# Attention a: statistics of two norms side by side, one GpSimd power for both, the second norm applied behind the maximum, the router later

## Chip, core and metric

One core of a Trainium2 chip runs the whole kernel. The metric is the device time of one execution in microseconds (us). Engines: PE is TensorE, PEld its weight loads, DVE is VectorE, ACT is ScalarE, POOL is GpSimd, SP is SyncE (here it only issues DMAs).

## What is computed

The input is 16 blocks of 256 tokens with 128 features. Four layers follow each other, each with a residual:

```
x = x + attn_a(layernorm(x))     # one head of width 128, rotary table, softmax over the 256 keys
x = x + ffn(layernorm(x))        # router: 8 experts, the best one per token, gate = its softmax value
x = x + attn_b(layernorm(x))     # 16 heads of width 64, causal
x = x + ffn(layernorm(x))        # the same experts again

def _layernorm(x, eps=1e-05):
    m, v = mean(x), var(x)
    return (x - m) / sqrt(v + eps)
```

## The kernel before

The kernel is written for each engine as one queue of instructions in program order, with semaphores between them. X holds all tokens on chip (128 tokens by 128 features a tile, two tiles a block). There are four stages: attention a with the router of the first expert layer (up to about 147 us), the experts, attention b with the second router, and the experts again.

Attention a is a software pipeline over the blocks. In turn s every engine runs its `attn_a(s, u)`, which does a different step for each of several blocks: the first norm (A) of block s, projections and rotary product of block s-1, scores, maximum and exponentials of s-2, transposed probabilities and output of s-3, residual and second norm (F) of s-4, the router of s-5. `has(b)` asks whether the block exists. Turns 0 to 7 are written out, 8 to 13 are a loop of two turns a round, then follow the routing of the first eight blocks (`route(0)`), turns 14 to 20, and the routing of the other eight (`route(1)`) with the experts.

The order in each queue in a turn of before:

- VectorE: residual of s-4 (L603); statistics (L558), aggregate (L565) and variance (L570) of norm A; the same of norm F; reciprocal of the row sums (L618); apply of A, called lnA, and of F, called lnF (both L581); rotation product (L630); maximum over the keys (L635); its scaling (L638); rotary sum (L644); router logits (L588).
- GpSimd: power -0.5 of A's variance, then of F's (L313), then the sine product of the rotary table (L351). In turns 14 to 19 each is followed by three scatters (L318) of routed tokens.
- ScalarE: copy of the transposed norm, xnT (L421); the router's copies TOK (L410) and fT (L413); copy of the transposed probabilities (L429); copy for the sine product (L434); two exponentials with row sums (L441); copy of the values, va (L449).
- TensorE: transposes of lnA (L902); router transposes of lnF (L885); transposes of the probabilities (L916); projections (L928); scores (L936); values (L943); output (L953); router products (L891).

In turns 17 to 20 a weight part is added: ScalarE casts (L488) and VectorE subtracts (L770).

`then_inc` raises a semaphore at an instruction's end, and `wait_ge` holds the whole queue of its engine. For instance, the second norm is applied under this wait:

```
b = s - 4
if has(b):
    norm_apply(LN["F"], b, TPB * b, u)     # dve.wait_ge(ln["s_rstd"], n + 1), two tensor_scalar
```

Of the kernel before, what the change touches and what calls it, by code (L numbers as in the profile page):

```python
# [111 lines left out]
def build(nc, ids, x, wqk_a, wv_a, rope, w_q, w_k, wv_b, w_o, W1, b1t, W2, b2, Wr, br, cst, out):  # L112
    ctx = ExitStack()
    with ctx:
# [17 lines left out]
        onesb = sb("onesb", [P, P], BF16)  # L132
        half = sb("half", [P, TPB])
        WQK = sb("WQK", [P, 4, D])
# [9 lines left out]

        LN = {}
        for n in "AFB":
            LN[n] = {
                "stats": sb(f"stats{n}", [P, 2, TPB, 6]), "mv": sb(f"mv{n}", [P, 2, TPB, 2]),
                "var": sb(f"var{n}", [P, 2, TPB]), "rstd": sb(f"rstd{n}", [P, 2, TPB]),
                "out": LN["A"]["out"] if n == "B" else sb(f"ln{n}", [P, 2, TPB, D]),  # L150
                "s_stats": sem(f"ln{n}_stats"), "s_mv": sem(f"ln{n}_mv"), "s_var": sem(f"ln{n}_var"),
                "s_rstd": sem(f"ln{n}_rstd"), "s_out": sem(f"ln{n}_out"),
            }
# [150 lines left out]
        def _(pool):  # L304
# [6 lines left out]
            def rstd(ln, n, slot):  # L311
                pool.wait_ge(ln["s_var"], n + 1)
                nc.gpsimd.tensor_tensor(ln["rstd"][:, slot, :], ln["var"][:, slot, :], half[:, :],  # L313
                                        ALU.pow).then_inc(ln["s_rstd"], 1)
# [25 lines left out]
            def attn_a(s, u):  # L340
                if has(s):
                    rstd(LN["A"], s, u)
                if has(s - 4):
                    rstd(LN["F"], s - 4, u)
                b = s - 1
                if has(b):
                    pool.wait_ge(a_qks, b + 1)
                    wait(pool, a_rope, b)
                    if fixed(b) and b == 0:
                        pool.wait_ge(s_wa, 48)  # L350
                    nc.gpsimd.tensor_tensor(rot[:, 1, :], qks[:, :], ROPE[:, 1, :], ALU.mult).then_inc(a_sin, 1)  # L351

            peeled(attn_a, 0, 8)
            turns(pool, attn_a, 8, 14)
            for s in range(14, NB + 5):
# [50 lines left out]
        def _(act):  # L406
# [8 lines left out]
            def attn_a(s, u):  # L415
                v = (u + 1) % 2
                b = s - 1
                if has(b):
                    act.wait_ge(a_xT_ps, b + 1)
                    wait(act, a_v_ps, b - 1)  # L420
                    nc.scalar.copy(xnT[:, v, :], PS[:, 4, 0:M]).then_inc(a_xT, 1)  # L421
                b = s - 5
                if has(b):
                    router_copies(b, TPB * b, v, 7)
                b = s - 3
# [20 lines left out]
                if has(b):  # L446
                    act.wait_ge(a_v_ps, b + 1)
                    wait(act, a_out_ps, b - 1)
                    nc.scalar.copy(va[:, v, :, :], PS[:, 5, 0:TPB * D].rearrange("p (t d) -> p t d", t=TPB)).then_inc(a_v, 1)  # L449

            def route(k):
# [80 lines left out]
            turns(act, attn_a, 14, 16)  # L532
            for s in range(16, NB + 5):
                attn_a(s, s % 2)
                if s >= NB + 1:
                    weight_parts(s - (NB + 1))
# [11 lines left out]
        def _(dve):  # L548
# [23 lines left out]

            def norm_stats(ln, n, tile, slot):
                bn_stats(ln, n, tile, slot)
                bn_aggr(ln, n, slot)
                norm_var(ln, n, slot)

            def norm_apply(ln, n, tile, slot):
                dve.wait_ge(ln["s_rstd"], n + 1)
# [12 lines left out]
            def attn_a(s, u):  # L592
# [14 lines left out]
                if has(s):  # L607
                    if not fixed(s) or s >= 2:
                        dve.wait_ge(a_xT_ps, s - 1)
                    norm_stats(LN["A"], s, TPB * s, u)  # L610
                if has(b):
                    dve.wait_ge(a_x, b + 1)
                    wait(dve, r_tok, b - 1)
                    norm_stats(LN["F"], b, TPB * b, u)
                b = s - 3
# [3 lines left out]
                if has(s):  # L619
                    norm_apply(LN["A"], s, TPB * s, u)  # L620
                b = s - 4
                if has(b):
                    norm_apply(LN["F"], b, TPB * b, u)
                b = s - 1
                if has(b):
# [3 lines left out]
                    wait(dve, a_rope, b)  # L629
                    nc.vector.tensor_tensor(rot[:, 0, :], PS[:, 0, :], ROPE[:, 0, :], ALU.mult).then_inc(a_rot, 1)  # L630
                b = s - 2
                if has(b):
# [4 lines left out]
                    dve.wait_ge(a_max, b + 1)  # L637
                    nc.vector.tensor_scalar(nba[:, u, :], mxa[:, u, :], -SCALE_A, None, ALU.mult).then_inc(a_nb, 1)  # L638
                b = s - 1
                if has(b):  # L640
# [4 lines left out]
                                            ALU.add).then_inc(a_rope, 1)  # L645
                b = s - 5
                if has(b):
                    if fixed(b) and b == 0:
                        dve.wait_ge(s_wr, 32)
                    logits(b, TPB * b, 7)  # L650

# [130 lines left out]
            def attn_b(s, u, p0=0, p1=NPAIR):  # L782
# [8 lines left out]
                for p in range(p0, p1):  # L791
# [26 lines left out]
                    if p == 4 and has(s):  # L818
                        norm_apply(LN["B"], s, TPB * s, u)
                    if p == 4 and has(fb):  # L820
# [9 lines left out]
                    if p == 5 and has(fb):  # L830
                        norm_apply(LN["F"], fb + NB, TPB * fb, u)
                    if has(b):
# [16 lines left out]
            turns(dve, attn_a, 14, 16)  # L849
            for s in range(16, NB + 5):  # L850
                attn_a(s, s % 2)
                if s >= NB + 1:
                    weight_parts(s - (NB + 1))
# [19 lines left out]
        def _(pe):  # L873
# [21 lines left out]
            def attn_a(s, u):  # L895
                v = (u + 1) % 2
                b = s - 1
                if has(b):
# [4 lines left out]
                    last.then_inc(a_xT_ps, 1)  # L903
                b = s - 5
                if has(b):
                    if fixed(b) and b == 0:
                        pe.wait_ge(s_wr, 32)
                    wait(pe, r_lg, b)
                    router_T(b, v, 7)
                b = s - 3  # L910
# [21 lines left out]
                if has(b):  # L932
                    pe.wait_ge(a_rope, b + 1)
                    wait(pe, a_exp, b)
                    for i in range(TPB):
                        last = mm(PS[:, 2, i * M:(i + 1) * M], qk[:, u, 0, i * P:(i + 1) * P], qk[:, u, 1, :],  # L936
                                  start=True, stop=True)
                    last.then_inc(a_scores, 1)
                b = s - 1
                if has(b):  # L940
# [6 lines left out]
                if has(b):  # L947
# [161 lines left out]
            turns(pe, attn_a, 14, 16)  # L1109
            for s in range(16, NB + 5):  # L1110
                attn_a(s, s % 2)
# [77 lines left out]
```

## Time and profile before

| | |
|---|---|
| median of 3 runs | 983.93 us (983.05 to 984.64) |
| profiled execution | 987.06 us |
| its span | 984.9 us |
| granted TensorE clock, mean | 0.934 |
| busy: PE, DVE, ACT, POOL | 86%, 66%, 57%, 45% |

The span runs from the first to the last instruction; the 2.2 us around it are start and end of the execution. In a row in order of time, the first number is the start in us from the span's start, the second the duration, and what stands in square brackets is the idle time of the engine before it with what ended it. "x2" means two instructions taken together. The name before the arrow is the tile written. XY and w1b are tiles that attention a borrows: XY holds probabilities and copies there, w1b the rotated products.

### The profile page before, as it was taken

The page shows a single profiled execution, that of the slowest core. Times are in us where ns is not written, and L with a number is a line of the kernel's source. Part 1 is how long each engine was busy: PE and PEld are TensorE (multiplying, and loading weights), DVE is VectorE, ACT ScalarE, POOL GpSimd, SP SyncE. Part 2 cuts the span into 40 slices and gives each one's busy share as a digit, 9 for nine tenths or more (in the row PEclk, how much of TensorE's full clock was granted, in tenths as well). Part 3 has the DMA queues.
Part 4 walks back from the last instruction along what each step waited for, and adds up shares of the span by engine and source line. Part 5 has one row for each costly group of instructions (what it writes and reads, how often), then busy time and mean ns, then how long its engine had stood idle before and what let it go on. Part 6 is the DMA issues. An engine that isn't in the chain of part 4 may idle for free. (4 is left out here: it accounts for less than half of the span.)

```text
span 984.9 us, 24722 instructions
## 1 busy us (share of the span) xinstructions
PE 843.6 (86%) x6756; PEld 706.2 (72%) x6756; DVE 645.8 (66%) x2713; ACT 557.7 (57%) x2089; POOL 441.0 (45%) x755
## 2 busy tenths in 40 slices
PE   5888665399979999999999979989999999538993
PEld 4676555399967778777877857867877787538993
DVE  4888866166647776776767687667667666615665
ACT  2444343166657766776676656666667666315661
POOL 3333362555534444443434424674444444074552
PEclk9999777599979999999999999999999999768996
DMA  9900012302010000000000000001000000021214
GB/s 335 320 14 0 9 36 78 105 32 78 32 52 2 1 2 2 2 2 2 1 2 1 0 1 2 18 29 62 0 1 0 0 2 1 4 99 41 78 35 144
DMA packets 25936, 40.05 MB, mean 41 GB/s; under 512 B 4656, under 2 KB 17584, under 8 KB 24816
## 3 DMA queue, kind: packets, MB, share of 16 engines
q1 hardware_dynamic: 20848, 28.76, 9.0%
q0 software_dynamic: 4992, 10.27, 3.2%
q8 instruction: 29, 0.48, 0.2%
q14 instruction: 67, 0.55, 0.2%
HBM read 20.58 MB, written 18.43 MB: 40 GB/s over the span
## 5 line engine op out<-in xcount | busy, mean ns | idle before, releaser
L378 POOL TENSOR_SCALAR pb<-pb,rib 128x128 f32<-128x128 f32 x256 | 96.0, 375 | 307.1 <-DVE rib L789 306.0
L804 DVE CUSTOM_DVE_ANT_0 PS<-PS,CST 128x128 f32<-128x128 f32 (+1 forms) x512 | 167.8, 389 | 62.0 <-PE PS L1022 49.6
L473 ACT ACTIVATE yT<-PS,w1b 128x128 f32<-128x128 f32 x368 | 105.3, 369 | 115.7 <-remote 48.1
L503 ACT COPY qk<-PS 128x512 f32<-128x512 f32 x128 | 75.1, 587 | 155.6 <-PE PS L880 155.6
L334 POOL DMA_INDIRECT yt_dram<-XY x92 | 97.8, 1063 | 82.0 <-DVE XY L737 78.4
L840 DVE COPY pT<-PS 128x384 f32<-128x384 f32 x256 | 130.6, 551 | 1.8 <-PE PS L1033 1.1
L1022 PE MATMUL PS<-qk 64*128 64x128 f32 (+1 forms) x1024 | 120.0, 353 | 8.2 <-ACT pb L520 6.6
L520 ACT ACTIVATE pb<-PS,nbb 128x256 f32<-128x256 f32 x256 | 125.3, 490 | 0.0
L380 POOL TENSOR_SCALAR pb<-pb,rib 128x256 f32<-128x256 f32 x256 | 123.2, 481 | 0.0
L1001 PE MATMUL PS<-yT 128*128 128x128 f32 x736 | 102.9, 285 | 20.8 <-ACT yT L473 12.8
L1033 PE MATMUL PS<-CST,pb 128*128 128x128 f32 x768 | 110.8, 277 | 10.8 <-POOL pb L380 9.9
L1043 PE MATMUL PS<-pT,vb 128*64 128x256 f32 (+1 forms) x1024 | 111.5, 339 | 0.0
L1001 PEld LDWEIGHTS PS<-yT 128*128 128x128 f32 x736 | 94.4, 201 | 22.3 <-ACT yT L473 13.8
L992 PE MATMUL PS<-pb,w1b 128*128 128x128 f32 x736 | 105.7, 290 | 0.2 <-issue 0.2
L518 ACT ACTIVATE pb<-PS,nbb 128x128 f32<-128x128 f32 x256 | 97.9, 382 | 9.3 <-DVE nbb L804 9.0
L1033 PEld LDWEIGHTS PS<-CST,pb 128*128 128x128 f32 x768 | 87.8, 143 | 17.7 <-POOL pb L380 17.4
L992 PEld LDWEIGHTS PS<-pb,w1b 128*128 128x128 f32 x736 | 96.6, 205 | 0.9 <-issue 0.3
L789 DVE RECIPROCAL rib<-rsb 128x2 f32<-128x2 f32 x256 | 40.9, 160 | 81.4 <-ACT pb L520 80.8
L737 DVE TENSOR_TENSOR XY<-PS,yT 128x128 f32 (+1 forms) x92 | 26.8, 292 | 98.6 <-PE PS L1001 48.6
L1043 PEld LDWEIGHTS PS<-pT,vb 128*64 128x64 f32 x1024 | 62.1, 136 | 40.3 <-issue 18.0
L1022 PEld LDWEIGHTS PS<-qk 64*128 64x128 f32 x1024 | 68.1, 188 | 31.2 <-issue 16.3
L878 PE MATMUL PS<-xh,WQKh 128*128 128x256 f32 x256 | 86.4, 338 | 2.3 <-DVE WVBl L856 2.3
(129 smaller groups left out, 1769.8 us busy)
## 6 DMA issues: line engine op xcount, KB each, us to landing
xs_dram<-XY SPq DMA_DIRECT2D x4, 1483.5 KB, 13.4
XY<-xs_dram SPq DMA_DIRECT2D x4, 1225.5 KB, 6.1
W1S<-in_W SPq DMA_DIRECT2D x1, 2048.0 KB, 20.9
W2S<-in_W SPq DMA_DIRECT2D x4, 512.0 KB, 7.7
out_dram<-X SPq DMA_DIRECT2D x8, 256.0 KB, 4.4
yt_dram<-XY POOLq DMA_INDIRECT x92
XY<-xs_dram SPq DMA_DIRECT2D x4, 258.0 KB, 2.7
xs_dram<-TOK,POS POOLq DMA_INDIRECT x64
```

The costliest lines, as they stand in the source:

```text
L334: nc.gpsimd.indirect_dma_start(out=yt_dram[k], out_offset=bass.IndirectOffsetOnAxis(ap=XY[:, tile, D:DI].bitcast(I32), axis=0), in_=XY[:, ...
L380: nc.gpsimd.tensor_scalar(pb[:, hh % 4, P:3 * P], pb[:, hh % 4, P:3 * P], rib[:, hh % 4, 1:2], 1.0, ALU.mult, ALU.mult).then_inc(b_p, 1)
L473: last = nc.scalar.activation(hT[:, v, c, :], PS[:, v, c * P:(c + 1) * P], ACT.Gelu, bias=w1b1[:, v, F + c:F + c + 1])
L518: nc.scalar.activation(pb[:, r, 0:P], PS[:, bank, 0:P], ACT.Exp, bias=nbb[:, r, 0:1], scale=-1.0, accum_out=rsb[:, r, 0:1])
L520: nc.scalar.activation(pb[:, r, P:3 * P], PS[:, bank, P:3 * P], ACT.Exp, bias=nbb[:, r, 1:2], scale=-1.0, accum_out=rsb[:, r, 1:2]).then_i ...
L804: last = nc.vector.tensor_tensor_reduce(ps, ps, CST[:, m:m + c1 - c0], -SCALE_B, HIGHEST, ALU.add, ALU.min, nbb[:, hh % 4, c0 // P:c0 // P ...
L840: nc.vector.tensor_copy(pT[:, hh % 4, :], PS[:, T_BANKS[i], 0:3 * P]).then_inc(b_pT, 1)
L992: last = mm(PS[:, v, c * P:(c + 1) * P], w1b1[:, v, c * P:(c + 1) * P], xsT[:, v, :], start=True, stop=True)
L1001: last = mm(PS[:, 6 + w, 0:D], hT[:, w, c, :], w2b2[:, r, c * D:(c + 1) * D], start=c == 0, stop=c == FC - 1)
L1022: last = mm(PS[:, S_BANKS[pair][i], c0:c0 + k1], qk[r, pair % 2, 0, q0:q0 + P], qk[r, pair % 2, 1, 0:k1], start=True, stop=True)
L1033: last = tr(PS[:, T_BANKS[i], c * P:(c + 1) * P], pb[:, hh % 4, c * P:(c + 1) * P], ident)
L1043: last = mm(PS[i * DK:(i + 1) * DK, AV_BANK, q0:M], vb[:, slot, c, hh * DK:(hh + 1) * DK], pT[:, hh % 4, k0:k1], start=c == 0, stop=c == 1 ...
```

## The change

On VectorE the statistics of A and F are followed by both aggregates and then both variances. GpSimd raises both variances to the power in one instruction over 128x4 elements (128x2 where only one norm is due), signalled by one semaphore, `a_rstd`. VectorE applies A as before behind it. F is applied behind the scaled maximum and in front of the rotary sum. The router moves: ScalarE's copies stand behind va and no longer behind xnT; TensorE's router transposes stand behind the scores, and its products one turn later (block s-6) in front of the transposes of the probabilities; the logits also come a turn later, between the rotation product and the maximum. So there is one more turn (21), and TensorE waits for `r_xT` before the first routing.

```diff
-        half = sb("half", [P, TPB])
+        half = sb("half", [P, 2 * TPB])
+        a_rstd = sem("a_rstd")
+        varAF, rstdAF = (sb(n, [P, 2, 2 * TPB]) for n in ("varAF", "rstdAF"))
...
             def attn_a(s, u):                      # GpSimd
-                if has(s):
-                    rstd(LN["A"], s, u)
-                if has(s - 4):
-                    rstd(LN["F"], s - 4, u)
+                if has(s) or has(s - 4):
+                    c = slice(0 if has(s) else TPB, 2 * TPB if has(s - 4) else TPB)
+                    if has(s):
+                        pool.wait_ge(LN["A"]["s_var"], s + 1)
+                    if has(s - 4):
+                        pool.wait_ge(LN["F"]["s_var"], s - 3)
+                    nc.gpsimd.tensor_tensor(rstdAF[:, u, c], varAF[:, u, c], half[:, c], ALU.pow).then_inc(a_rstd, 1)
...
-                b = s - 5                          # ScalarE, behind xnT
-                if has(b):
-                    router_copies(b, TPB * b, v, 7)
...
+                b = s - 5                          # ScalarE, behind va
+                if has(b):
+                    router_copies(b, TPB * b, v, 7)
...
                 if has(s):                         # VectorE
-                    norm_stats(LN["A"], s, TPB * s, u)
+                    bn_stats(LN["A"], s, TPB * s, u)
                 if has(b):
                     dve.wait_ge(a_x, b + 1)
-                    wait(dve, r_tok, b - 1)
-                    norm_stats(LN["F"], b, TPB * b, u)
+                    bn_stats(LN["F"], b, TPB * b, u)
+                if has(s):
+                    bn_aggr(LN["A"], s, u)
+                if has(b):
+                    bn_aggr(LN["F"], b, u)
+                if has(s):
+                    norm_var(LN["A"], s, u)
+                if has(b):
+                    norm_var(LN["F"], b, u)
...
                 if has(s):
-                    norm_apply(LN["A"], s, TPB * s, u)
-                b = s - 4
-                if has(b):
-                    norm_apply(LN["F"], b, TPB * b, u)
+                    norm_apply(LN["A"], a_rstd, s + 1, TPB * s, u)
...
+                b = s - 6                          # behind the rotation product
+                if has(b):
+                    logits(b, TPB * b, 7)
...
+                b = s - 4                          # behind the scaled maximum
+                if has(b):
+                    wait(dve, r_tok, b - 1)
+                    norm_apply(LN["F"], a_rstd, s + 1, TPB * b, u)
...
-                b = s - 5                          # last in the turn
-                if has(b):
-                    logits(b, TPB * b, 7)
...
-                b = s - 5                          # TensorE, behind the transposes of lnA
+                b = s - 6
                 if has(b):
-                    wait(pe, r_lg, b)
-                    router_T(b, v, 7)
+                    router(b, u, 7)
...
+                b = s - 5                          # behind the scores
+                if has(b):
+                    wait(pe, r_lg, b)
+                    router_T(b, v, 7)
...
-                b = s - 5                          # last in the turn
-                if has(b):
-                    router(b, v, 7)
...
+                if k == 0:                         # TensorE, route(k)
+                    pe.wait_ge(r_xT, GB + 1)
...
-            for s in range(16, NB + 5):
+            for s in range(16, NB + 6):
```

## Rows read from the trace of the kernel before

**Rows 1.** The page, part 1: busy us, share of the span, instructions

```profile
PE 843.6 (86%) x6756; PEld 706.2 (72%) x6756; DVE 645.8 (66%) x2713; ACT 557.7 (57%) x2089; POOL 441.0 (45%) x755
```

**Rows 2.** Busy time by stretch: length, PE, PEld, DVE, ACT, POOL, PEclk, DMA share, GB/s

```profile
55.60:98.00 42.40, 34.99 (x210) 29.83 (x210) 37.19 (x133) 18.78 (x59) 15.17 (x18) 0.96 0.00 1
...
123.00:147.50 24.50, 15.33 (x86) 13.10 (x85) 14.84 (x54) 11.18 (x30) 16.43 (x18) 0.79 0.11 35
```

**Rows 3.** Order of time, VectorE: the scaled maximum of turns 3 and 13

```profile
26.98 0.19 DVE L638 TENSOR_SCALAR nba<-mxa 128x2 f32<-128x2 f32 x1
...
97.70 0.17 DVE L638 TENSOR_SCALAR nba<-mxa 128x2 f32<-128x2 f32 x1
```

**Rows 4.** Order of time, VectorE, turn 8 to 9

```profile
61.88 0.17 DVE L638 TENSOR_SCALAR nba<-mxa 128x2 f32<-128x2 f32 x1
...
63.20 0.48 DVE L558 BATCH_NORM_STATS2 statsA<-X 128x6 f32 x2
...
65.18 0.17 DVE L570 TENSOR_SCALAR varF<-mvF 128x2 f32<-128x2 f32 x1
...
65.33 0.58 DVE L581 TENSOR_SCALAR lnA<-X,mvA,rstdA 128x128 f32 x2
...
66.24 1.46 DVE L581 TENSOR_SCALAR lnF<-X,mvF,rstdF 128x128 f32 x2 [0.33 <-POOL rstdF L313]
...
67.62 0.68 DVE L630 TENSOR_TENSOR w1b<-PS,ROPE 128x512 f32<-128x512 f32 x1
...
68.93 0.17 DVE L638 TENSOR_SCALAR nba<-mxa 128x2 f32<-128x2 f32 x1
```

**Rows 5.** Order of time, GpSimd, the same turn

```profile
64.36 0.69 POOL L313 TENSOR_TENSOR rstdA<-varA,half 128x2 f32<-128x2 f32 x1 [3.79 <-DVE varA L570]
...
65.43 0.78 POOL L313 TENSOR_TENSOR rstdF<-varF,half 128x2 f32<-128x2 f32 x1 [0.38 <-DVE varF L570]
...
66.53 1.09 POOL L351 TENSOR_TENSOR w1b<-XY,ROPE 128x512 f32<-128x512 f32 x1 [0.32 <-ACT XY L434]
```

**Rows 6.** Order of time, TensorE and ScalarE, the same turn

```profile
60.66 0.51 PE L891 MATMUL PS<-WRS,fT 128*128 128x8 f32 x4
...
63.13 0.37 ACT L449 COPY va<-PS 128x256 f32<-128x256 f32 x1
...
63.29 0.66 PE L916 MATMUL PS<-CST,XY 128*128 128x128 f32 x4
63.39 0.39 ACT L421 COPY xnT<-PS 128x256 f32<-128x256 f32 x1
63.65 0.43 ACT L410 COPY TOK<-lnF 128x256 f32 x1
...
63.83 1.99 PE L928 MATMUL PS<-xnT,WQK 128*128 128x256 f32 x8
63.96 0.40 ACT L413 COPY fT<-PS 128x256 f32<-128x256 f32 x1
...
65.66 1.03 PE L936 MATMUL PS<-qk 128*128 128x256 f32 x4
```

**Rows 7.** Order of time, turn 13, in which L351 comes late

```profile
92.39 3.48 PE L928 MATMUL PS<-xnT,WQK 128*128 128x256 f32 x8
...
94.80 0.60 DVE L581 TENSOR_SCALAR lnF<-X,mvF,rstdF 128x128 f32 x2 [0.33 <-POOL rstdF L313]
```

**Rows 8.** Order of time, VectorE: an aggregate right behind its statistics

```profile
71.13 0.25 DVE L565 BATCH_NORM_AGGREGATE mvA<-statsA 128x2 f32<-128x6 f32 x2 [0.15 <-DVE statsA L558]
```

**Rows 9.** Order of time: turns 14 and 15, and the second routing's first step

```profile
113.93 0.17 DVE L638 TENSOR_SCALAR nba<-mxa 128x2 f32<-128x2 f32 x1
...
116.28 3.62 PE L928 MATMUL PS<-xnT,WQK 128*128 128x256 f32 x8
...
121.66 0.17 DVE L638 TENSOR_SCALAR nba<-mxa 128x2 f32<-128x2 f32 x1
...
147.56 0.28 DVE L671 TENSOR_REDUCE r_mx<-LG 128x16 f32<-128x128 f32 x1
```

**Rows 10.** Waits from 140 to 205 us: in total, times, longest

```profile
ACT yT L473 <- remote: 24.4, 2, 15.5
```

More of the change, by code:

```diff
@@ L148, in build @@
                 "stats": sb(f"stats{n}", [P, 2, TPB, 6]), "mv": sb(f"mv{n}", [P, 2, TPB, 2]),
-                "var": sb(f"var{n}", [P, 2, TPB]), "rstd": sb(f"rstd{n}", [P, 2, TPB]),
+                "var": sb("varB", [P, 2, TPB]) if n == "B" else varAF[:, :, "AF".index(n) * TPB:("AF".index(n) + 1) * TPB],
+                "rstd": sb("rstdB", [P, 2, TPB]) if n == "B" else rstdAF[:, :, "AF".index(n) * TPB:("AF".index(n) + 1) * TPB],
                 "out": LN["A"]["out"] if n == "B" else sb(f"ln{n}", [P, 2, TPB, D]),
@@ L312, in rstd @@
                 pool.wait_ge(ln["s_var"], n + 1)
-                nc.gpsimd.tensor_tensor(ln["rstd"][:, slot, :], ln["var"][:, slot, :], half[:, :],
+                nc.gpsimd.tensor_tensor(ln["rstd"][:, slot, :], ln["var"][:, slot, :], half[:, 0:TPB],
                                         ALU.pow).then_inc(ln["s_rstd"], 1)
@@ L354, in _ @@
             turns(pool, attn_a, 8, 14)
-            for s in range(14, NB + 5):
+            for s in range(14, NB + 6):
                 attn_a(s, s % 2)
@@ L532, in _ @@
             turns(act, attn_a, 14, 16)
-            for s in range(16, NB + 5):
+            for s in range(16, NB + 6):
                 attn_a(s, s % 2)
-                if s >= NB + 1:
+                if NB + 1 <= s < NB + 5:
                     weight_parts(s - (NB + 1))
@@ L571, in norm_var, with norm_apply @@
                                         ALU.add).then_inc(ln["s_var"], 1)
[L573 to L579, printed above, removed]
+            def norm_apply(ln, s_rstd, count, tile, slot):
+                dve.wait_ge(s_rstd, count)
                 for i in range(TPB):
@@ L630, in attn_a @@
                     nc.vector.tensor_tensor(rot[:, 0, :], PS[:, 0, :], ROPE[:, 0, :], ALU.mult).then_inc(a_rot, 1)
+                b = s - 6
+                if has(b):
+                    if fixed(b) and b == 0:
+                        dve.wait_ge(s_wr, 32)
+                    logits(b, TPB * b, 7)
                 b = s - 2
@@ L645, in attn_a @@
                                             ALU.add).then_inc(a_rope, 1)
-                b = s - 5
-                if has(b):
-                    if fixed(b) and b == 0:
-                        dve.wait_ge(s_wr, 32)
-                    logits(b, TPB * b, 7)
             def route(k, between=None):
@@ L818, in attn_b @@
                     if p == 4 and has(s):
-                        norm_apply(LN["B"], s, TPB * s, u)
+                        norm_apply(LN["B"], LN["B"]["s_rstd"], s + 1, TPB * s, u)
                     if p == 4 and has(fb):
@@ L830, in attn_b @@
                     if p == 5 and has(fb):
-                        norm_apply(LN["F"], fb + NB, TPB * fb, u)
+                        norm_apply(LN["F"], LN["F"]["s_rstd"], fb + 1, TPB * fb, u)
                     if has(b):
@@ L849, in _ @@
             turns(dve, attn_a, 14, 16)
-            for s in range(16, NB + 5):
+            for s in range(16, NB + 6):
                 attn_a(s, s % 2)
-                if s >= NB + 1:
+                if NB + 1 <= s < NB + 5:
                     weight_parts(s - (NB + 1))
@@ L1109, in _ @@
             turns(pe, attn_a, 14, 16)
-            for s in range(16, NB + 5):
+            for s in range(16, NB + 6):
                 attn_a(s, s % 2)
```

## Prediction

> **What bounds the kernel now.** I read the page first. TensorE is busy for 86% of the span and VectorE for 66% [rows 1], but these are averages over four stages, and the change lies in one of them, attention a, in the first 147 us. So the next view is the table by stretch: from 55.60 to 98.00 VectorE is busy 37.19 of 42.40 us and TensorE 34.99 [rows 2]. Then comes the order of time of one turn of the loop over the blocks. I write N(s) for the end of the scaled maximum (L638) in turn s. N(3) is 27.17 and N(13) is 97.87 [rows 3]: ten turns in 70.70 us, 7.07 each. In the turn from 61.88 to 68.93 the longest idle time of VectorE is 0.33 us [rows 4]. The scores are ready at 66.69 (L936 in [rows 6]); the scaling starts at 68.93 and the maximum before it takes 0.71, so the maximum reads them 1.5 us after they are ready. VectorE is the bound of a steady turn; the chain through ScalarE and TensorE has some slack.
>
> One VectorE row is far too long: the second norm's apply (lnF) takes 1.46 us, the first norm's (lnA, the same work) 0.58 [rows 4]. GpSimd's product L351 runs from 66.53 to 67.62 [rows 5], and lnF ends at 67.70. In the turn in which L351 comes late, lnF takes 0.60 [rows 7]. So lnF loses 0.8 us in most turns by running beside L351.
>
> **Part by part: VectorE alone.** (1) Statistics side by side. From statsA at 63.20 to the end of varF at 65.35 it is 2.15 us [rows 4], with short gaps behind each dependent step; a row elsewhere shows one as 0.15 idle [rows 8]. With A's and F's alternating, each result is ready when it is wanted. Now F's own chain is the path: A's statistics 0.40 (rows overlap the next by 0.08), F's 0.48, the 0.15, the aggregates 0.25, 0.03, the variance 0.17, which is 1.48 us: 0.67 gained, and nothing at the least. I take 0.67, since the gaps stand in the rows. (2) One power for both. Before, A's power (0.69) lay beside F's statistics and F's (0.78) beside lnA, with 0.33 us left bare [rows 4, 5]. Now nothing but a 0.16 us reciprocal lies beside it, so it is bare: 0.11 of handoffs and the power P. A power over 128x4 isn't in the trace. Its bounds are 0.69 (as over 128x2) and 1.47 (two of them). L351 multiplies 128x512 in 1.09 us, only 0.4 more than a power of two columns, so most of it is fixed and I take P = 0.80. (3) lnF behind the maximum: it starts at N + 0.02, when L351 is over, and takes 0.60 and not 1.46. VectorE's turn, by difference: 7.07; less 0.67 of (1); plus 0.93 between the end of varF and the start of lnA (0.11 + P + 0.02, as they touched before); less 0.39, as lnA's follower comes 0.52 and not 0.91 after its start; less 0.86, as lnF's follower comes 0.52 and not 1.38 after its start [rows 4]. That is 6.08 us, or 5.28 + P.
>
> The Trainium skill speaks against (1). "VectorE: DVE Perf Modes", section "Rules for kernel authors", says that chained operations drain whatever one does, and to reduce their count, not their semaphores. The count stays the same, so by the page (1) gains nothing; the row with 0.15 us of idle is against it. By the page VectorE's turn would be 6.75 and not 6.08.
>
> **The chain that takes over.** The router is moved too, and that is what decides. Its ScalarE copies (TOK, fT) went behind xnT; now they go behind va, and so in front of the next turn's xnT. TensorE's router products for block s-6 now stand in front of the transposes of the probabilities, and wait for that fT. The chain from one maximum to the next, from the starts in [rows 6]: N to va 1.01 (1.08 in this turn, whose first handoff of 0.17 is the longest; 0.03 to 0.17), va to TOK 0.26 (as to xnT), TOK to fT 0.31, fT 0.40, handoff 0.05, router products 0.37 (0.51, less the overlap with the next), transposes L916 0.54, L928 1.83 (63.83 to 65.66), scores 1.03, handoff 0.04, maximum 0.71, scaling 0.17. The sum is 6.72; I take 6.77 for the slower handoffs of the loop. Before, L928 started 1.78 after N and now 2.94: the same chain was 1.2 us shorter, 5.5, and was hidden. Queued behind the waiting router products are L916, L928, the scores and the whole of TensorE's turn. The router transposes wait for logits(s-6), but after the scores, off this chain. So of the 0.99 us that VectorE gains, 0.30 reach the turn: 8 turns (6 to 13) x 0.30 = 2.4 us.
>
> Turns 4 and 5 have no router products. Turn 4, with no lnF before it, takes 6.08 - 0.52 = 5.6 on VectorE and not 7.0: 1.4. In turn 5 L351 is early and meets lnA instead: nothing. With 0.2 for the uneven turns of before, 4.0 us at N(13), between 2.5 and 6.
>
> **Turns 14 to 21.** Turn 14 follows the routing (8.6 us of VectorE), during which L351's input is already there. So GpSimd starts L351 right behind the power, beside lnA, and lnA pays what lnF paid: nothing is gained (0.0 to 0.8). In turn 15 TensorE runs at half clock: L928 takes 3.62 and not 1.99 [rows 9], and N(14) = 114.10 to N(15) = 121.83 is 7.73. The new chain there is 6.77 + 1.63 + 0.5 (router products and transposes at half clock) = 8.9, so 0.9 to 1.2 is lost. The window 123.00 to 147.50 has a granted clock of 0.79 [rows 2], so the scores of turn 17 find the same insertion in front of them: 1.1 lost. In turn 17 lnF waits for the last maximum, and the residual, the statistics and the residual of the next turn queue behind it: 0.6 lost, which nothing hides, as no new block comes in. In the last turn the logits come one turn later (one more fT, 1.02 of router products at half clock, less the 0.6 of a weight part that now lies in front): 0.5. GpSimd's scatters are issued in the same number between its steps; one instruction fewer is no gain there. The sum for turns 14 to 21 is 3.1 us lost (2 to 4.5).
>
> Net at the start of the second routing: 4.0 - 3.1 = 0.9 us earlier. Behind it everything hangs on this start: the routing, 16 scatters, the experts. One more term: the chain has no slack left for half clock in steady turns. Before, L928 took 3.48 once in ten turns [rows 7] and cost the turn only 0.2; now one costs 1.5 to 2. I subtract 0.4 for a window that may come. That leaves 0.5 us. The profiled execution took 987.06 us (span 984.9), so its like would take 986.6; the median of the runs is 983.93, 0.3% lower, and the same 0.5 us gives **983.4 us**.
>
> **Rivals.** A, the forecast: the router in TensorE's queue eats most of VectorE's gain and the tail the rest: 983.4, own range 981.5 to 985.5, chance 0.42.
> B, the chain is shorter than summed: if fT is there before TensorE wants it, the turn goes down to 6.4, or to VectorE's own 6.1. Beyond the forecast eight turns then gain 3.0 to 5.4, so 980.4 down to 978.0. For it: ScalarE is the emptiest of the three here (18.78 of 42.40 busy). Against it: the in-order queues above. Chance 0.28.
> C, slower: TensorE's clock. In the stretch of the routing and after it the granted clock is down, and TensorE's waits there are long; if two of turns 6 to 13 get a half-clock stretch on L928, each costs 1.5 + 0.5, where before slack of 1.4 took it. Then 983.4 + 4 = 987.4; from one such turn more than forecast, the kernel is slower. Against it: TensorE's share of a turn rises from 83% to 86%, and 9 of 10 turns ran at full clock. Chance 0.18.
> D, VectorE stays the bound: P near 1.1 or more and nothing gained from side by side give 5.28 + 1.1 + 0.67 = 7.05, so the steady turns gain nothing and only turn 4 is left: 983.9 + 3.1 - 1.0 = 986.0. Chance 0.12, since the rows have the gaps. By the rule of the Trainium skill above (VectorE: DVE Perf Modes) its second half would be certain.
> On top of each lies the stretch after the second routing, where ScalarE waits 24.4 us for something the trace doesn't name [rows 10], while the scatters run. It moves with the start; how its length answers to a shift of a microsecond I can't say, and I give it 1.5 us either way. That the change doesn't do what it says isn't a case: one power for two and lnF's place are plain in the code.
>
> **How the numbers follow.** The likeliest is A: 983.4. A measurement of this kernel can tell about 0.2% (2.0 us) from no change. A is split 0.06 faster, 0.32 same, 0.04 slower; B 0.27 and 0.01 same; C 0.02 same and 0.16 slower; D 0.06 same and 0.06 slower. Together: faster 0.33, same 0.41, slower 0.26. The range takes A, the nearer part of B, D, and C to about its middle: 979.5 to 987.4; the ends of B and C are left out.
>
> **What would show it.** Right: steady turns of 6.7 to 6.9 us; lnF at 0.6 behind the scaling; a power of 128x4 near 0.8, followed by lnA; VectorE idle in front of the rotation (L630) by about 0.4, released by TensorE's L928; TensorE idle in front of the router products, released by ScalarE's fT; lnA near 1.3 in turn 14; the second routing's start within 2 us of 147.56 [rows 9]. Wrong: turns of 6.2 (B), L928 rows above 3 us in turns 6 to 13 (C), VectorE without idle at 7 us a turn (D), or a stretch behind the second routing that changed its length by more than the start moved.

## The result, and the profile after

| | median, us | runs | ratio to before |
|---|---|---|---|
| before | 984.28 | 983.05 to 985.10 | |
| after | 990.08 | 989.72 to 992.47 | 1.0065 [1.0049, 1.0082] |

The change makes the kernel 5.8 us slower. The prediction was 983.4 us with a range to 987.4, so it missed on the slow side. The profiled executions differ by less: after's took 989.72 us (span 987.8), before's 987.06 (span 984.9), which is 3 us above before's median. Two executions of kernels below that took far longer than their likes (2049 us of the router alone, 1360 us of the norms at ten places less) are left out of the ratios.

The page, part 1, and two of its stretches by the table by window (length, then busy us of PE, PEld, DVE, ACT and POOL, granted clock, DMA share, GB/s), to be set beside [rows 1, 2]:

```profile
PE 851.6 (86%) x6756; PEld 712.3 (72%) x6756; DVE 635.4 (64%) x2713; ACT 559.0 (57%) x2089; POOL 435.6 (44%) x743
...
54.00:95.60 41.60, 35.30 (x226) 29.80 (x226) 33.54 (x137) 19.91 (x61) 13.65 (x13) 1.00 0.00 1
123.00:147.50 24.50, 16.12 (x90) 13.61 (x90) 14.42 (x56) 11.49 (x31) 16.22 (x17) 0.76 0.14 44
```

VectorE is busy for 10 us less in all, and in the steady turns for 33.54 of 41.60 us, where it had 37.19 of 42.40. Its steady turns went as forecast. This is one of its turns in order of time (start, duration, idle time before with what ended it), first VectorE, then GpSimd, TensorE and ScalarE; it answers to [rows 4 to 6]:

```profile
61.49 0.34 DVE L649 TENSOR_SCALAR nba<-mxa 128x2 f32<-128x2 f32 x1
61.75 0.59 DVE L583 TENSOR_SCALAR lnF<-X,mvF,rstdAF 128x128 f32 x2
...
63.38 0.47 DVE L565 BATCH_NORM_STATS2 statsA<-X 128x6 f32 x2
...
64.67 0.17 DVE L577 TENSOR_SCALAR varAF<-mvF 128x2 f32<-128x2 f32 x1
...
65.96 0.60 DVE L583 TENSOR_SCALAR lnA<-X,mvA,rstdAF 128x128 f32 x2 [1.06 <-POOL rstdAF L351]
66.78 0.69 DVE L636 TENSOR_TENSOR w1b<-PS,ROPE 128x512 f32<-128x512 f32 x1 [0.23 <-PE PS L937]
...
68.37 0.19 DVE L649 TENSOR_SCALAR nba<-mxa 128x2 f32<-128x2 f32 x1
...
64.91 1.01 POOL L351 TENSOR_TENSOR rstdAF<-varAF,half 128x4 f32<-128x4 f32 x1 [3.10 <-DVE varAF L577]
...
63.92 0.61 PE L901 MATMUL PS<-WRS,fT 128*128 128x8 f32 x4 [1.02 <-ACT fT L420]
...
63.17 0.42 ACT L417 COPY TOK<-lnF 128x256 f32 x1
63.48 0.39 ACT L420 COPY fT<-PS 128x256 f32<-128x256 f32 x1
```

The turn takes 6.73 us (61.83 to 68.56), forecast 6.77. From statsA to the end of varF it is 1.46 us, forecast 1.48. lnF is short and stands behind the scaling. TensorE is idle for 1.02 us until fT is there. Only the power is off: 1.01 us over 128x4, where I took 0.80.

Turn 6 ran at half clock, and turn 14 behaved as forecast. These are the rotation product and scaling of turn 6 with their projections and scores, then lnA of turn 14, the scalings of turns 14 and 15, and the start of the second routing, which answers to [rows 9]:

```profile
46.15 0.69 DVE L636 TENSOR_TENSOR w1b<-PS,ROPE 128x512 f32<-128x512 f32 x1 [2.64 <-PE PS L937]
48.32 0.17 DVE L649 TENSOR_SCALAR nba<-mxa 128x2 f32<-128x2 f32 x1
...
42.49 3.62 PE L937 MATMUL PS<-xnT,WQK 128*128 128x256 f32 x8
45.91 1.65 PE L945 MATMUL PS<-qk 128*128 128x256 f32 x4
...
108.49 1.36 DVE L583 TENSOR_SCALAR lnA<-X,mvA,rstdAF 128x128 f32<-128x128 f32 x2 [1.12 <-POOL rstdAF L351]
111.17 0.17 DVE L649 TENSOR_SCALAR nba<-mxa 128x2 f32<-128x2 f32 x1
...
121.28 0.20 DVE L649 TENSOR_SCALAR nba<-mxa 128x2 f32<-128x2 f32 x1
...
147.17 0.29 DVE L681 TENSOR_REDUCE r_mx<-LG 128x16 f32<-128x128 f32 x1
```

N(13) is 95.51, 2.4 us earlier than before, and the second routing starts at 147.17, 0.4 us earlier than before [rows 9]. Of this 1.3 us were there at N(3), 25.91 and not 27.17, ahead of the first turn that has a second norm, and N(3) lies between 25.9 and 28.9 in all traces of this document. Counted from N(3), the second routing starts 0.9 us later than before. The loss of 5.8 us is not in this stage.

**Where it is.** Attention b forms a tile xl once a block (L794 before, L804 after). Its start in both traces, from block to block, dates the loss. In the rows of before, then of after, the line between two xl is the first VectorE instruction behind the jump back of attention b's loop:

```profile
654.04 0.40 DVE L794 TENSOR_TENSOR xl<-PS,xh 128x256 fp32r<-128x256 f32 x1
662.00 0.30 DVE L804 CUSTOM_DVE_ANT_0 PS<-PS,CST 128x128 f32<-128x128 f32 x1 [2.98 <-issue]
690.64 0.42 DVE L794 TENSOR_TENSOR xl<-PS,xh 128x256 fp32r<-128x256 f32 x1 [0.47 <-ACT xh L527]
724.61 0.42 DVE L794 TENSOR_TENSOR xl<-PS,xh 128x256 fp32r<-128x256 f32 x1 [0.47 <-ACT xh L527]
731.08 0.30 DVE L804 CUSTOM_DVE_ANT_0 PS<-PS,CST 128x128 f32<-128x128 f32 x1 [2.85 <-issue]
759.74 0.42 DVE L794 TENSOR_TENSOR xl<-PS,xh 128x256 fp32r<-128x256 f32 x1 [0.47 <-ACT xh L527]
```

```profile
653.52 0.40 DVE L804 TENSOR_TENSOR xl<-PS,xh 128x256 fp32r<-128x256 f32 x1
662.39 0.30 DVE L814 CUSTOM_DVE_ANT_0 PS<-PS,CST 128x128 f32<-128x128 f32 x1 [3.92 <-issue]
692.59 0.42 DVE L804 TENSOR_TENSOR xl<-PS,xh 128x256 fp32r<-128x256 f32 x1 [0.47 <-ACT xh L534]
726.62 0.42 DVE L804 TENSOR_TENSOR xl<-PS,xh 128x256 fp32r<-128x256 f32 x1 [0.47 <-ACT xh L534]
734.13 0.30 DVE L814 CUSTOM_DVE_ANT_0 PS<-PS,CST 128x128 f32<-128x128 f32 x1 [3.90 <-issue]
764.32 0.42 DVE L804 TENSOR_TENSOR xl<-PS,xh 128x256 fp32r<-128x256 f32 x1 [0.47 <-ACT xh L534]
```

At 654 after is 0.52 us ahead. In these rows it takes 34.0 us from one xl to the next in both kernels where no jump lies between. Where one does, before takes 36.60 and 35.13 and after 39.07 and 37.70. At 764 after is 4.58 us behind. The instruction behind the jump waits for no semaphore ("issue"): 2.98 and 2.85 us before, 3.92 and 3.90 after. So each jump has 1 us more of VectorE's wait, but costs 2.5 us. Behind both jumps TensorE's granted clock, 1.00 in the windows of before, is 0.83 in those of after, a mean over rows at full (2.4 GHz) and at half clock (1.2). The first experiment has a long wait without the fall of the clock, and tells the two apart.

```profile
664.00:674.00 10.00, 10.00 (x89) 8.03 (x90) 7.58 (x36) 6.60 (x27) 4.75 (x12) 1.00 0.43 153
...
734.00:744.00 10.00, 10.00 (x88) 8.37 (x88) 7.58 (x40) 5.96 (x23) 5.03 (x12) 1.00 0.00 1
```

```profile
664.00:674.00 10.00, 9.73 (x72) 8.32 (x74) 6.49 (x32) 6.11 (x26) 3.33 (x8) 0.83 0.42 153
...
734.00:744.00 10.00, 8.00 (x56) 6.70 (x57) 6.53 (x33) 5.07 (x21) 3.32 (x8) 0.83 0.01 2
```

The fourth routing (that of the last eight blocks in the second expert layer) starts at 844.88 before and at 849.88 after, 5.0 us later. Behind it, 2.1 us come back in the profiled execution, where ScalarE's waits "ACT yT <- remote" are 23.7 us in before's trace and 17.3 in after's. The medians, 5.8 apart, don't show this return.

Attention b's code is the same in both kernels, but for the number that one wait counts to and the place of a few small tiles. What changed is where its code lies. A trace also has the records of instructions that no view shows (semaphores, registers, branches), so they can be counted. The body of this loop is 406 VectorE instructions in every trace, some 1950 instructions into the queue, and ten instructions further on in the changed kernel. The norms' half brings the ten: with the router's half alone the loop stands where it did.

Attention b has this body in two loops, one for turns 4 to 7 and one for turns 10 to 15, and the two jumps are those of the second. The first loop has one jump back, some 770 instructions earlier in the queue. Its wait didn't grow with the same shift. Before, then after:

```profile
445.68 0.30 DVE L804 CUSTOM_DVE_ANT_0 PS<-PS,CST 128x128 f32<-128x128 f32 x1 [3.05 <-issue]
```

```profile
444.94 0.30 DVE L814 CUSTOM_DVE_ANT_0 PS<-PS,CST 128x128 f32<-128x128 f32 x1 [2.96 <-issue]
```

So ten instructions more don't lengthen every jump back: it depends on where the loop stands.

### The profile page after: what moved, and what is told of

Same layout as the page of the kernel before. It is cut to its first block and busy times, and to the rows that moved or that the text cites. A ratio compares the mean times of both kernels' runs of the same rounds, so it can differ in the third digit from the quotient of the medians.

```text
span 987.8 us, 24728 instructions
## 1 busy us (share of the span) xinstructions
PE 851.6 (86%) x6756; PEld 712.3 (72%) x6756; DVE 635.4 (64%) x2713; ACT 559.0 (57%) x2089; POOL 435.6 (44%) x743
```

## The experiments

The theory: the loss is the place of VectorE's code, not attention a. The rivals: attention a's change acts on through buffers and start times, or one of its halves is the cause. "Places" are VectorE instructions ahead of attention b's second loop, counted against the kernel before. They are made with increments of the semaphore `dve_waited`, for which no engine waits.

### Code moved and nothing else

```diff
         def _(dve):
+            for _ in range(10):
+                dve.sem_inc(dve_waited)
             dve.wait_ge(s_cst, 16)
```

> The kernel before, with ten semaphore increments added at the very start of VectorE's queue, where it waits for its constants anyway; they only shift VectorE's later instructions by ten places, as the change does. Theory P (the place of VectorE's code sets what a jump back in its 406-instruction loop of attention b costs): the same stall as after the change, 3.9 us and not 2.9 at each of two jumps, then TensorE at half clock, about +5 us, so 989. Theory A (attention a's new order does it, in its effect on later stages): no change, 984.

Measured: 991.47 us against 984.16, ratio 1.0087 [1.0061, 1.0112]. VectorE waits 4.04 and 4.01 us at the jumps:

```profile
663.17 0.30 DVE L806 CUSTOM_DVE_ANT_0 PS<-PS,CST 128x128 f32<-128x128 f32 x1 [4.04 <-issue]
...
733.38 0.30 DVE L806 CUSTOM_DVE_ANT_0 PS<-PS,CST 128x128 f32<-128x128 f32 x1 [4.01 <-issue]
```

Ten instructions without any effect make the kernel before as slow as the changed one. The two jump rounds account for 3.7 us here (37.63 + 37.83 against 36.60 + 35.13). The rest of the 7.3 us isn't located: the profiled execution shows only 2.9 us in all.

The two rounds also tell the wait from the clock. The first costs 1.03 us more, just the longer wait, and TensorE keeps its full clock behind it. The second costs 2.70, and there the clock falls:

```profile
664.00:674.00 10.00, 8.96 (x80) 7.33 (x80) 7.74 (x38) 7.31 (x30) 3.77 (x10) 1.00 0.43 153
...
734.00:744.00 10.00, 8.75 (x63) 7.29 (x64) 6.67 (x34) 5.79 (x23) 3.30 (x8) 0.83 0.00 1
```

### The change without the shift

```diff
+            spare = [11]
+
+            def mark():
+                if spare[0] > 0:
+                    spare[0] -= 1
+                else:
+                    dve.sem_inc(dve_waited)
...
-                dve.sem_inc(dve_waited)        # in bn_stats and bn_aggr
+                mark()
```

> The changed kernel with eleven of VectorE's bookkeeping semaphore increments left out in the first turns, so that from the first expert stage on VectorE's instructions stand at the same places as in the kernel before. Theory P: the two stalls shrink back, attention b costs what it did, and 983 to 984.5 comes out, the time forecast for attention a alone. Theory A: still 989 to 990.

Measured: 983.23 us, ratio 1.0001 [0.9984, 1.0019], waits of 2.90 and 2.98. Its trace has ten VectorE instructions fewer than that of the changed kernel (4972 and 4982), so the loop stands at place 0. The steady turns take 6.72 to 6.75 us, as in the changed kernel. So attention a's change by itself is worth nothing that can be measured, and 983.23 is near the 983.4 that the prediction had said of it.

### The two halves, both without the shift

Norms alone (one power, side by side, lnF behind the maximum, router where it was), with eleven increments left out as above. Against the changed kernel:

```diff
-                b = s - 6                      # TensorE, in front of the transposes
+                b = s - 5
                 if has(b):
-                    router(b, u, 7)
+                    wait(pe, r_lg, b)
+                    router_T(b, v, 7)
...
+                    router(b, v, 7)            # last in the turn
```

> Only the norms' half of the change (statistics side by side, one power, second norm behind the maximum), router as before, code places as before. My theory: without the router's delay GpSimd's sine product starts 4.5 us after the scaled maximum and meets the first norm's apply (VectorE gets there at 4.3), which takes 1.36 and not 0.60: turns of about 7.0 us as before, no extra turn and no loss at the end, 982 to 984.5. Rival: there is no such meeting, VectorE's own 6.3 us a turn, about 977.

Measured: 978.88 us, ratio 0.9942 [0.9922, 0.9962]. In the loop the turns take 6.22 to 6.36 us, with lnA at 0.60: the rival was right there. My collision is real, but it is found in the written-out turns and in turn 14. Here lnA meets GpSimd's sine product:

```profile
53.06 1.45 DVE L591 TENSOR_SCALAR lnA<-X,mvA,rstdAF 128x128 f32<-128x128 f32 x2 [1.12 <-POOL rstdAF L351]
...
53.34 1.09 POOL L358 TENSOR_TENSOR w1b<-XY,ROPE 128x512 f32<-128x512 f32 x1 [0.32 <-ACT XY L441]
```

The router alone: the norms' steps as before, two powers included, and the router's copies, transposes, products and logits in their new places:

```diff
+                    norm_apply(LN["F"], LN["F"]["s_rstd"], b + 1, TPB * b, u)   # right behind lnA
...
-                    norm_apply(LN["F"], a_rstd, s + 1, TPB * b, u)              # behind the scaling
```

> Only the router's half (copies behind va, products one turn later in front of the transposes of the probabilities, one more turn), norms as before, code places as before. My theory: the chain through fT and the router products takes 6.77 us and pushes the sine product behind the second norm's apply, which falls from 1.4 to 0.60: turns of 6.8 us, the same 3 us lost in turns 14 to 21, so 983 to 985. Rival: the router's delay adds to VectorE's turn, 7.1 or more, 986 to 988.

Measured: 988.2 us, ratio 1.0043 [1.0028, 1.0058], just above the rival's 986 to 988. The loop's turns are those of my theory, 6.81 to 6.92 us with lnF at 0.60. What it had too small is the end: N(13) to the second routing takes 53.86 us and took 49.69, 4.2 lost and not 3. (The second routing starts at 151.17, 3.6 us later than before, but 1.7 of this is there at N(3).) So the norms bring 5.3 us, and the router's new place takes 4.0.

### Better versions: sine product later, router behind the projections

The norms' half with one wait more on GpSimd, in front of the sine product, for the first norm's output; then the same ten places earlier; then the changed kernel (aligned) with TensorE's router products moved behind the projections. These three ran on a second chip, on which the kernel before takes 937.22 us, so their ratios are to be compared and not their times.

```diff
+                    if has(s):
+                        pool.wait_ge(LN["A"]["s_out"], s + 1)      # GpSimd, in front of L358
```

> norm_only, and GpSimd's sine product waits until the first norm is applied (lnA done), so that the two can't meet. Code places as before. My theory (the first turns of norm_only, 7.0 to 7.25 us, are the sine product beside lnA at 1.38 us): all turns from 4 on take 6.3 us, lnA 0.60 throughout, turn 14 too; 4 to 5 us less than norm_only, 974 to 976. Rival (those turns are long for another reason, such as TensorE's clock or the input's transfers): turns 4 to 8 stay at 7 us and the time at 979.

Measured: 924.58 us, ratio 0.9862 [0.9843, 0.9882]. Turns 5 to 13 take 6.20 to 6.36 us, N(13) is 89.06, and lnA is 0.60 throughout, in turn 14 too:

```profile
49.31 0.61 DVE L593 TENSOR_SCALAR lnA<-X,mvA,rstdAF 128x128 f32<-128x128 f32 x2 [1.12 <-POOL rstdAF L351]
...
50.09 1.09 POOL L360 TENSOR_TENSOR w1b<-XY,ROPE 128x512 f32<-128x512 f32 x1 [0.81 <-DVE lnA L593]
```

GpSimd waits 0.81 us for lnA, and nobody waits for GpSimd. From N(3) to the second routing it takes 108.17 us, and 112.78 in the norms alone: 4.6 less, as my theory had it. This is the best version found, 1.4% faster than the kernel before. That is more than the 1.0% at most of my theory, and the two ran on different chips.

```diff
-            spare = [11]
+            spare = [21]
```

> norm_late_sine with ten more of VectorE's bookkeeping increments left out, so that its later code stands ten places earlier than in the kernel before. If the stall at the jump grows evenly with the place (0.1 us for each), it is 1.9 us here and the kernel 2 to 5 us faster than norm_late_sine; if the place matters only as a step between 0 and +10, it stays at 2.9 us and nothing changes.

Measured: 924.72 us, ratio 0.985 [0.9835, 0.9865], waits of 2.87 and 2.85: ten places earlier change nothing.

```diff
                 b = s - 6
                 if has(b):
-                    router(b, u, 7)        # in front of the transposes of the probabilities
...
+                    router(b, u, 7)        # behind the projections
```

> The changed kernel at the code places of before (as after_skip11), with TensorE's router products behind the projections and no longer in front of the transposes of the probabilities. My theory (the wait for fT in TensorE's queue is part of the chain): steady turns of 6.4 and not 6.75 us, some 3 to 5 us less than after_skip11, 979 to 981. Rival (the turn is bound by VectorE, or by the ScalarE copies in front of xnT alone): turns of 6.75, 983.

Measured: 931.79 us, ratio 0.9937 [0.9921, 0.9952]. Turns 6 to 13 take 6.45 to 6.71 us, not 6.73, and turn 6 has no half clock (turn 5 has some, and takes 6.99). Where TensorE waits for fT it is the chain, as the prediction had it, and the way out is to let it work on projections meanwhile.

### Does the other chip have the waits?

```diff
-            for _ in range(10):
+            for _ in range(20):                # and 5, 8, 15 and 26 in the kernels named so
```

> The kernel before with twenty increments at the start of VectorE's queue. Even growth with the place: stalls of 4.9 us at the two jumps of VectorE's loop in attention b, about 994. A step between 0 and +10: 4.0 us as with ten.

Measured, in one execution: 936.57 us, no slower than the 937.22 of the kernel before. I first looked for the jumps near 669 us, found no wait, and took it that this chip has none. The next expectations still leave this open, and it was wrong: the kernel is 25 us ahead by then, and the jumps lie at 636 and 706.

```profile
636.42 0.30 DVE L806 CUSTOM_DVE_ANT_0 PS<-PS,CST 128x128 f32<-128x128 f32 x1 [3.09 <-issue]
...
705.63 0.30 DVE L806 CUSTOM_DVE_ANT_0 PS<-PS,CST 128x128 f32<-128x128 f32 x1 [2.87 <-issue]
```

So twenty places give the short wait again, and neither the 4.9 nor the 4.0 us of the expectation: the first sign that the wait doesn't simply grow. The next four ran on a third chip, where the kernel before takes 937.54 us.

> The changed kernel once more. My theory: its loss against the kernel before comes from attention b's two jumps back on VectorE, where the wait for code grew from 2.98 and 2.85 to 3.92 and 3.90 us. So where the kernel before takes about 984 us and shows those waits, the ratio is 1.005 to 1.008 again; where it takes about 937 us and they are not there, the ratio is that of attention a alone, 0.997 to 1.001. The rival, that something in the experts' blocks or in attention a itself makes the loss, expects 1.005 or more in both.

Measured: 942.74 us, ratio 1.0052 [1.0038, 1.0066], waits of 4.15 and 3.95. The loss is there as on the first chip. The expectation's 0.997 to 1.001 was for a chip without the waits, and this one has them. By its ratio alone this run would speak for the rival; the waits in its trace and the next runs don't.

> The kernel before with ten more increments of a semaphore at VectorE's start, so that all its later code lies ten places on. Where the jumps of attention b show waits for code of about 3 us: 1.006 to 1.010, with the waits at about 4 us. Where they do not: 0.999 to 1.001, as the place of the code then costs nothing. A rival, that the ten instructions cost by themselves or upset the order of the start, expects over 1.003 in both.

Measured: 941.45 us, ratio 1.0033 [1.002, 1.0045], waits of 4.07 and 3.89. The waits are as expected, the ratio is less than the 1.006 named, and by itself it would suit the rival too. The loss is 3.9 us, and its jump rounds are 3.7 us longer than in the kernel with five places (75.39 and 71.72): here the jumps are nearly the whole of it. Again the clock stays full behind the first jump, whose round is 1.1 us longer, and falls at the second, 2.6 us longer.

> The same with five increments in place of ten. Where the waits at the jumps are about 3 us in the kernel before: if the wait grows evenly with the place of the code, about 3.5 us and a ratio near 1.004; if it grows in one step, either 3 us and 1.000 or 4 us and 1.008. Where there are no such waits: 0.999 to 1.001, and the question stays open.

Measured: 938.02 us, ratio 1.0004 [0.999, 1.0017], waits of 2.99 and 2.85. Five places cost nothing; no even growth from 0 to 10.

> The half of the change that concerns the norms, router left where it was, code places behind attention a as before. It shortens attention a by about 7 us in the loop's turns (7.07 to 6.25 us a turn) and loses some of it behind. Ratio 0.992 to 0.996 where the kernel before takes 984 us; where it takes 937 us, 0.989 to 0.994, since less of the lead is lost in waits for code behind the second routing.

Measured: 931.05 us, ratio 0.993 [0.9917, 0.9944]. The norms' half holds on both kinds of chip.

### Ten places more

> The changed kernel with ten increments of a semaphore added at VectorE's start, so that attention b's loop lies twenty places behind that of the kernel before. If the loss is only the place of that loop, and twenty places give back the short wait, the waits at the two jumps back are 2.85 to 3.1 us and the ratio is 0.997 to 1.002: a kernel with more instructions is 5 us faster. The rival, that the wait grows or stays long with more places, expects 3.9 us or more and a ratio of 1.005 to 1.010.

The changed kernel with the ten increments of the first experiment, on a fourth chip, as the three that follow. Measured: 986.04 us against 984.21, ratio 1.0016 [0.9998, 1.0035]:

```profile
661.53 0.30 DVE L816 CUSTOM_DVE_ANT_0 PS<-PS,CST 128x128 f32<-128x128 f32 x1 [3.02 <-issue]
...
731.05 0.30 DVE L816 CUSTOM_DVE_ANT_0 PS<-PS,CST 128x128 f32<-128x128 f32 x1 [2.88 <-issue]
```

More instructions, and the ratio falls from 1.0065 to 1.0016. In front of the jumps this kernel and the changed one stand alike (xl at 653.54 and 653.52); behind them it is 4.5 us ahead (759.79 and 764.32). Together with the first two experiments that settles where the loss is and that the code's place makes it.

> The kernel before with eight increments in front. Read for the wait at the two jumps back of attention b alone. If the long wait belongs to a band of places that starts between 5 and 10, it is either 2.9 to 3.1 or 3.9 to 4.1 us; if the wait grew evenly from 5 to 10 places, about 3.6 us.

Measured: waits of 2.93 and 2.81. The round of the first jump is still 1.2 us longer than before's, with a clock of 0.89 from 655 to 665: here the loss goes with the clock alone, without a longer wait.

> The kernel before with fifteen increments in front. The wait at the two jumps is 3.9 to 4.1 us if the band of long waits reaches fifteen places, 2.9 to 3.1 us if it ends before.

Measured: waits of 3.26 and 3.27, neither of the two values I had named.

> The kernel before with 26 increments in front. If the wait repeats with a period of 16 places, 26 is like 10: 3.9 to 4.1 us at the two jumps. If it doesn't, 2.9 to 3.1 us.

Measured: 992.7 us in one execution. The waits at the jumps are 2.91 and 3.08, but two instructions on comes a second one:

```profile
659.37 0.30 DVE L806 CUSTOM_DVE_ANT_0 PS<-PS,CST 128x128 f32<-128x128 f32 x1 [2.91 <-issue]
...
661.43 0.43 DVE L806 CUSTOM_DVE_ANT_0 PS<-PS,CST 128x256 f32<-128x256 f32 x1 [1.70 <-issue]
```

The shifted kernels together, with the time of both jump rounds from xl to xl, and the wait at the first loop's one jump:

| places | kernel | waits at the two jumps | both rounds, us | wait, first loop |
|---|---|---|---|---|
| -10 | norms, sine later | 2.87, 2.85 | 71.69 | 3.07 |
| 0 | before | 2.98, 2.85 | 71.73 | 3.05 |
| 0 | the change, aligned | 2.90, 2.98 | 71.79 | 2.95 |
| 5 | before | 2.99, 2.85 | 71.72 | 2.96 |
| 8 | before | 2.93, 2.81 | 72.87 | 3.13 |
| 10 | before | 4.04, 4.01 | 75.46 | 2.94 |
| 10 | before, third chip | 4.07, 3.89 | 75.39 | 2.91 |
| 10 | after | 3.92, 3.90 | 76.77 | 2.96 |
| 10 | after, third chip | 4.15, 3.95 | 77.18 | 2.95 |
| 15 | before | 3.26, 3.27 | 72.39 | 3.41 |
| 20 | before | 3.09, 2.87 | 72.06 | 3.06 |
| 20 | after | 3.02, 2.88 | 72.22 | 3.11 |
| 26 | before | 2.91 + 1.70, 3.08 + 1.79 | 80.05 | 2.97 + 1.36 |

The wait grows in no simple way with the place, and it doesn't repeat every sixteen places. Why it is long at 10 in the one loop and not in the other, and split at 26 in both, stays open. Nor is the place all of it: in the kernel with the router behind the projections, which stands at place 0, the first loop's jump waited 3.62 us.

## Why the prediction was wrong

**The step that failed** is the last of "Turns 14 to 21": "Behind it everything hangs on this start", with "1.5 us either way" for the stretch of [rows 10]. I asked how the code behind attention a answers to a shift in time, and never how it answers to a shift in place. The start of that stretch moved by 0.4 us, ScalarE's two waits there took 23.6 us and had taken 24.4, and the lead was there still at 654 us (0.52). Then two jumps back took 5.0 us more than before. The trace of before had the jumps with nearly 3 us of "issue" in front of them; I had read no row behind 205 us. Without this step the time comes out: the aligned change took 983.23, forecast 983.4. But the sum behind it was only partly good, and its errors cancelled, as the parts below show.

**VectorE alone.** (1) Side by side: right, 1.46 against 1.48 us. The Trainium skill's rule ("VectorE: DVE Perf Modes", section "Rules for kernel authors") is to cut the number of chained operations, since they drain whatever one does. From it the prediction had worked out that side by side would gain nothing, and the 1.46 us are against that. (2) The power: mis-sized, 1.01 and not 0.80. It leaves VectorE idle for 1.03 to 1.12 us and puts VectorE's own turn at 5.28 + 1.01 = 6.29. With the norms alone, without the router's move, it is 6.22 to 6.36. (3) lnF behind the maximum: right, 0.60.

**The chain** (case A): right, 6.72 to 6.75 us in turns 8 to 13 against 6.77, released as said by fT and then by the projections. Its in-order part was the price: with the router products behind the projections, 6.45 to 6.71; without the router's move, 6.3. So B's 6.1 to 6.4 was no shorter chain but another kernel.

**Half clock** (case C): mis-sized, and not the chance that I took it for. I took 0.4 us for "a window that may come". Turn 6 alone took 9.77 us, 3.0 more than a steady turn, and not the 1.5 to 2 I had given, since the scores were slow too (1.65). In the four traces of the changed kernel with the router in this place, turn 6 takes 9.77, 8.32, 9.71 and 8.32 us, with 2.78 to 3.62 us of L937 and not 1.99. In the eight traces of the kernel before and its shifted versions, L928 of turn 6 takes 1.99 every time. Why the change brings it there wasn't tried. Turns 4 to 13 gained 1.1 us in all (69.60 from N(3) to N(13), and 70.70 before), below my lower end of 2.5; without turn 6's 3.0 it would be 4.1, forecast 4.0.

**Turns 14 to 21.** In all, N(13) to the second routing takes 51.66 us and took 49.69: 2.0 lost, at the lower end of 2 to 4.5. Turn 14 was right (lnA 1.36), and so was the last stretch behind N(17), 1.1 lost. Turn 15 lost 2.4 and not 0.9 to 1.2, turn 16 gained 1.1, and the 1.1 us that turn 17 was to lose didn't come. That the second routing starts 0.4 us earlier, near the forecast 0.9, is luck: N(3) came 1.3 us early in this execution. From there on the change lost 0.9 us, and 0.65 in the aligned kernel, where 0.5 was to be gained. That this difference isn't seen between 983.23 and 983.4 is luck too: the interval of that ratio is 1.8 us wide to either side.

**D** had nearly its first half (P 1.01, it named 1.1) and not its second, and the turns gained 0.33 us. C's time of 987.4 is nearest to the outcome, but its mechanism is not the cause: a forecast of "slower" by C would have been right for a wrong reason.

## What to carry to other kernels

A change that adds or removes instructions moves all code behind it on the same engine. Look in the trace of before for loops whose first instruction behind the jump waits for "issue", and price them before the change: here the same code waited 2.9 or 3.9 us at a jump, and that 1 us more cost 1.0 to 1.1 us where TensorE kept its clock and 2.5 to 2.8 where it fell. Before a small loss is put down to an edit, run the edit with its instruction count made up, and the old kernel with the same shift; and before a step is moved in one engine's queue, ask what that queue could do while it waits.

## What was not expected of the hardware

**Jumps back.** VectorE waits 2.8 to 4.2 us at each jump back of a loop of 406 instructions, by where the loop lies (at 26 places the wait comes in two parts, 4.6 us and more in the second loop). The Trainium skill ("Runtime: NRT & Kernel Launch", section "Instruction fetch mechanics") says that a taken branch to code outside the small window that is held forces a fetch of it. Every jump back of this loop that was read agrees with that; the page says nothing of a length that changes with the place, as on one chip between 5 places (2.99) and 10 (4.07).

**Two speeds of the same program.** The kernel before took 984 us on two of the chips and 937 on two others. Half of the difference lies between the second and the third routing (432.9 us in the trace of before, 408.3 in that of the kernel with twenty places more, which ran on a chip of the fast kind), and half behind the fourth (140.0 and 114.9). From 147 to 200 us TensorE is busy for 26.53 us in the trace of before (the first row), and for 47.70 in the other (the second).

```profile
147.00:200.00 53.00, 26.53 (x158) 24.02 (x159) 20.37 (x72) 13.93 (x50) 22.44 (x24) 0.64 0.25 87
```

```profile
147.00:200.00 53.00, 47.70 (x391) 46.36 (x392) 37.01 (x122) 31.67 (x119) 29.56 (x30) 0.89 0.26 92
```

ScalarE's 24.4 us for "remote" [rows 10] are not among the long waits there. What makes them on one chip and not on the other wasn't tried. Ratios held on both: 1.0065 and 1.0052 for the change, 0.9942 and 0.993 for the norms alone.

**VectorE beside GpSimd.** lnA takes 0.60 us alone and 1.36 to 1.50 when it meets GpSimd's product over 128x512, and one wait on GpSimd takes the collision away.
